# The first attention of a fused four-layer network: front work of a group of images moved beside the units of the group before

## The reference, cut to what matters

```python
q = grouped_proj(query, Wq).reshape(b, s, N_HEAD, D_HEAD) * SCALE
k = grouped_proj(query, Wk, bk).reshape(b, s, N_HEAD, D_HEAD)
v = grouped_proj(query, Wv, bv).reshape(b, s, N_HEAD, D_MODEL // N_HEAD)
content_score = jnp.einsum('bind,bjnd->bnij', q + r_w_bias * SCALE, k)
r_head = jnp.einsum('td,dnh->tnh', position_embeds, r_kernel)
pos_score = jnp.einsum('bind,tnd->bnit', q + r_r_bias * SCALE, r_head)
pos_score = rel_shift_gather(pos_score, s, shift=1)
attn_prob = jax.nn.softmax(content_score + pos_score, axis=-1)
attn_vec = jnp.einsum('bnij,bjnd->bind', attn_prob, v).reshape(b, s, D_MODEL)
h = query + (attn_vec @ Wo + bo)
mu = jnp.mean(h, axis=-1, keepdims=True)
var = jnp.mean(jnp.square(h - mu), axis=-1, keepdims=True)
return (h - mu) * jax.lax.rsqrt(var + EPS) * gamma + beta
```

## Time and profile before

| what | value |
|---|---|
| median of 3 runs | 1729.89 us (1724.44 to 1731.71) |
| the profiled execution, its own time | 1731.45 us |
| its span | 1729.6 us |
| TensorE busy with matmuls | 1444.7 us (84% of the span) |
| VectorE, ScalarE, GpSimd busy | 683.8, 669.8, 379.3 us |
| mean granted TensorE clock | 0.895 of full speed |

### The profile page before, as it was taken

How to read it: one execution, slowest core, us unless ns; L and a number is a source line. 1 busy time by engine, 2 the same in 40 slices (tenths; PEclk the granted TensorE clock), 3 DMA queues, 4 the chain that set the end, 5 groups by cost and what they waited for, 6 DMA issues and landing times.

```text
span 1729.6 us, 31842 instructions
## 1 busy us (share of the span) xinstructions
PE 1444.7 (84%) x10300; PEld 1045.9 (60%) x10300; DVE 683.8 (40%) x2107; ACT 669.8 (39%) x2209; POOL 379.3 (22%) x456
## 2 busy tenths in 40 slices
PE   6888788467687768788899899789999999889994
PEld 4555555343222335566667889656666777689994
DVE  5545655631101156544442722244442423461113
ACT  2666766120000033577753112145555542213331
POOL 5212212100000022322210156411211200024441
PEclk9898998568767868899999989989999999989997
DMA  8522523619999530000000566400000020026553
GB/s 216 142 70 69 138 60 79 223 42 345 319 305 287 166 103 1 1 0 0 0 0 0 137 194 197 142 6 1 0 0 0 5 123 0 19 75 205 184 174 101
DMA packets 94432, 178.64 MB, mean 103 GB/s; under 512 B 35578, under 2 KB 54168, under 8 KB 92704
## 3 DMA queue, kind: packets, MB, share of 16 engines
q1 hardware_dynamic: 80144, 130.65, 26.1%
q10 hardware_dynamic: 7056, 30.67, 5.5%
q0 software_dynamic: 7136, 16.10, 2.9%
HBM read 150.39 MB, written 26.99 MB: 103 GB/s over the span
## 4 chain that ended last, share of the span: by engine, by line
PE 55%; issue 14%; DMA 12%; DVE 10%; ACT 5%; SPq 2%; POOL 1%; DVEq 0%; ACTq 0%; POOLq 0%
PE bank L1762 14%; DMA WM<-in_fc 8%; PE bank L2231 6%; PE bank L2217 4%; PE bank L1852 4%; PE bank L1864 4%; PE bank L1881 3%; PE bank L1891 3%; PE bank L2221 3%; PE bank L1941 2%; PE bank L1828 2%; ACT ON L1573 1%; PE bank L2148 1%; DMA pos_scratch<-AREA 1%; ACT PB L1573 1%
## 5 line engine op out<-in xcount | busy, mean ns | idle before, releaser
L1762 PE MATMUL bank<-XT,AREA 96*128 96x408 f32 (+1 forms) x640 | 238.3, 530 | 33.4 <-ACT XT L1527 16.1
L1762 PEld LDWEIGHTS bank<-XT,AREA 96*128 96x128 f32 (+1 forms) x640 | 121.4, 196 | 139.3 <-issue 99.6
L1852 PE MATMUL bank<-KZ,QT 128*102 128x102 f32 x1152 | 145.8, 268 | 16.3 <-ACT PB L1573 6.3
L645 POOL TENSOR_TENSOR RS<-VE,expo 102x4 f32<-102x4 f32 (+1 forms) x53 | 53.0, 1000 | 433.7 <-DVE VE L855 325.6
L1852 PEld LDWEIGHTS bank<-KZ,QT 128*102 128x102 f32 x1152 | 126.5, 180 | 31.7 <-issue 13.6
L661 POOL TENSOR_TENSOR PB<-PB,RCU 102x306 f32<-102x306 f32 x96 | 66.8, 696 | 288.0 <-DVE RCU L916 287.7
L2231 PE MATMUL bank<-WM,KZ 128*128 x660 | 118.2, 327 | 0.0
L2231 PEld LDWEIGHTS bank<-WM,KZ 128*128 128x128 f32 x660 | 105.7, 190 | 0.4
L1554 ACT ACTIVATE KZ<-bank,AREA 128x128 f32<-128x128 f32 x198 | 54.6, 374 | 121.8 <-PE bank L2221 121.8
L1864 PE MATMUL bank<-AREA,OT 128*102 128x192 f32 x384 | 88.4, 343 | 15.4 <-DVE SLOTS L1133 5.4
L1881 PE MATMUL bank<-PT,V 102*32 102x102 f32 (+1 forms) x1152 | 86.0, 270 | 16.2 <-DVE OT L926 13.3
(11 more groups left out here) (312 smaller groups left out, 2769.7 us busy)
## 6 DMA issues: line engine op xcount, KB each, us to landing
AREA<-in_fc SPq DMA_DIRECT2D x10, 1536.0 KB, 20.2
SLOTS<-in_m3w SPq DMA_DIRECT2D x33, 384.0 KB
WM<-in_fc ACTq DMA_DIRECT2D x5, 2304.0 KB, 19.6
WM<-in_fc SPq DMA_DIRECT2D x6, 1536.0 KB, 19.5
AREA<-in_fc ACTq DMA_DIRECT2D x4, 2304.0 KB, 20.5
SLOTS<-in_m1w SPq DMA_DIRECT2D x33, 256.0 KB
AREA<-pos_scratch SPq DMA_DIRECT2D x16, 459.0 KB
pos_scratch<-AREA SPq DMA_DIRECT2D x8, 913.5 KB
```

Source lines behind the costliest of these rows:

```text
L1762: last = pe.matmul(dst, lhsT, rhs, start=n == 0, stop=n == len(pieces) - 1)
L1852: last = pe.matmul(psum[k][0:T, cols(j)], QT[:, tile, cols(bb)], KALL[:, unit % per_tile * (HEADS // per_tile) + tile, cols(bb)], start=Tr ...
```

## The change

Rows, queries and the position products of the first two images of the next group are made beside the units of this group, and its keys in the steps after the last unit's scores:

- step 6: the transposes of XN, and XT; steps 7, 8 and 9: two query tiles each; steps 10 to 15: two pairs of position products each (images 0 and 1 of the next group); steps 16, 17 and 18: two key tiles each. All of it goes through the two banks `XBANKS`.
- Only QR is made out of the bank. QT can't be overwritten while scores are still to be made, so VectorE makes it in steps 16 to 18 from QR, by adding a column of differences (`DQ`, the scaled r_w less r_r). `queries_ready` tells TensorE.
- TensorE waits for `scores_taken` (VectorE's add has read the bank) where it waited for `exp_ready`.
- `begin_a0`, `turn_a0` and `keep_a0` stand at steps 2, 4 and 6. GpSimd takes the power of the layer norm ahead of unit 2's probabilities, not unit 4's.
- `finish_0(g-1)` comes behind the move of V and ahead of the units.
- Each load of position scores waits for `pos_used`, now signalled by a marker instruction behind the add.
- The first group's front is written out ahead of the loop; the last group has nothing beside its units but its own images 2 and 3. What is left between two groups is `front()`: the values, and the waits for the keys' banks and for `queries_ready`.

The core of the diff:

```diff
+TURN_AHEAD, QUERIES_AHEAD, POS_AHEAD, KEYS_AHEAD = 6, (7, 8, 9), (10, 11, 12, 13, 14, 15), (16, 17, 18)
...
@@ SyncE
-                    if bb < 2:
-                        sp.wait_ge(sem["pos_used"], at.now("pos_used"))
-                    else:
-                        sp.wait_ge(sem["pos_used"], at.take("pos_used"))
+                    sp.wait_ge(sem["pos_used"], at.take("pos_used"))
...
@@ GpSimd
-                probabilities((4,))
+                probabilities((2,))
...
@@ VectorE, minima
+                    give(ins, "scores_taken")
+                    dve.wait_ge(sem["scores_taken"], at.now("scores_taken"))
                     if unit == UPB - 1:
-                        give(ins, "pos_used")
-                        dve.wait_ge(sem["pos_used"], at.now("pos_used"))
-                    else:
-                        step(ins)
+                        mark("pos_used")
...
@@ VectorE, between
+                        if s == 2:
+                            begin_a0(g + 1)
                         if s == 4:
-                            begin_a0(g + 1)
+                            turn_a0(g + 1)
                         if s == 6:
-                            turn_a0(g + 1)
-                        if s == 8:
                             keep_a0(g + 1)
...
+                        if s in QUERIES_AHEAD:
+                            queries_ahead(2 * QUERIES_AHEAD.index(s))
...
+                        if s in KEYS_AHEAD:
+                            keys_ahead(2 * KEYS_AHEAD.index(s))
...
+            def keys_ahead(first):
+
+                for p in (first, first + 1):
+                    last = ts(QT[:, p, :], QR[:, p, :], DQ[:, p:p + 1], None, ALU.add)
+                if first == 4:
+                    give(last, "queries_ready")
+                for p in (first, first + 1):
+                    keys(p)
...
             for g in range(NG):
                 at.first_banks()
...
+                values(V, 16, bv0)
                 if g:
                     finish_0(g - 1)
-                for p in range(6):
-                    keys(p)
-                values(V, 16, bv0)
                 attention(16, True, lambda bb, o, k: free(tt(a_of(g)(bb), o, a_of(g)(bb), ALU.add), k),
                           between_groups(g))
...
@@ ScalarE
+            def beside_ahead(s):
+
+                beside(s)
+                if s == TURN_AHEAD:
+                    turned(XT)
+                if s in QUERIES_AHEAD:
+                    for p in range(2 * QUERIES_AHEAD.index(s), 2 * QUERIES_AHEAD.index(s) + 2):
+                        queries(p)
+                if s in POS_AHEAD:
+                    pos_rows(POS_AHEAD.index(s) // 3, 2 * (POS_AHEAD.index(s) % 3), 2)
+                if s in KEYS_AHEAD:
+                    for p in range(2 * KEYS_AHEAD.index(s), 2 * KEYS_AHEAD.index(s) + 2):
+                        keys(p)
...
+            with at.loop(act, NG - 1):
+                attention(beside_ahead)
+            attention(beside)
...
@@ TensorE
-                            pe.wait_ge(sem["exp_ready"], at.take("exp_ready"))
+                            pe.wait_ge(sem[scores_read], at.take(scores_read))
...
+                    if s == TURN_AHEAD:
+                        pe.wait_ge(sem["xn_ready"], at.take("xn_ready"))
+                        turned.extend(turn_group(XN, halves))
+                        fresh.append(True)
+                    if s in QUERIES_AHEAD:
+                        n = 2 * QUERIES_AHEAD.index(s)
+                        if n == 0:
+                            moved(*turned)
+                        q.extend(project(wq0, p6) for p6 in (n, n + 1))
+                    if s in POS_AHEAD:
+                        n = POS_AHEAD.index(s)
+                        if n == 0:
+                            moved(*q[2:4])
+                        if n == 2:
+                            moved(*q[4:6])
+                        pos(n // 3, 2 * (n % 3), 2)
+                    if s in KEYS_AHEAD:
+                        n = 2 * KEYS_AHEAD.index(s)
+                        for p6 in (n, n + 1):
+                            project(wk0, p6)
...
+            def front():
...
+                for k in XBANKS:
+                    pe.wait_ge(sem[f"bank_free{k}"], at.now(f"bank_full{k}") + 1)
+                pe.wait_ge(sem["queries_ready"], at.take("queries_ready"))
+                return v_moved
...
+            with at.loop(pe, NG - 1):
+                v_moved = front()
+                attention(2, 16, wo0, v_moved, beside_ahead())
+            v_moved = front()
+            attention(2, 16, wo0, v_moved, beside)
```

189 lines of the change are left out of this document (97 added, 92 removed).

## The result

The changed kernel takes 1740.24 us (median of 20 runs, 1732.51 to 1745.85) against 1729.79 us (20 runs, 1720.76 to 1739.88) of the kernel before: a ratio of 1.005, 95% interval 1.0034 to 1.0065. It is slower by 10.5 us; the prediction said faster by 8.7.

The account below looks back on a forecast made before the run. Bound taken: a store-and-load chain of position scores, about 10.5 us, ending the wait at each group's start. Three periods gave -8.2 us, with -1.0 and +0.5 -8.7: 1721.2 us from a median of 1729.89; range 1707 to 1736.

Parts of the forecast that it names:

- A: Last output projection's start to the next group's second position-product batch: +12.3 in place of +24.9 us, -12.6.
- B: Second batch of position products to the scores of unit 6: +0.5 us on 12.4.
- C: Scores of unit 6 to unit 10, with transposes and query products added: 11.6 us against 9.9, +1.7.
- D: Unit 10 to unit 15, with position pairs added: 2.6 us a step, 13.0 against 10.0, +3.0.
- E: Drain, unit 15's scores to the last output projection: 14.1 us against 8.2, +5.9; bounds +2.3 and +7.5.
- the forecast case: Whole kernel: change of -2 to -15 us, time 1715 to 1728 us; chance 0.50.
- R2: Slow TensorE clock enters steps 6 to 10 or 16 to 18: +19.5 us, 1741 us; chance 0.20.
- The first front: First group's front, two banks and no overlap of queries with products: +0.5 us, between 0 and +2.
- The wait for scores: TensorE may write scores once VectorE has read the bank: -1.0 us in the last group, bounds 0 and -3.
- QT: VectorE's six SBUF passes a group making QT: 0.6 us each, bounds 0.37 and 0.64.

Follow-up runs that it names:

- e_finish: Changed kernel with the second layer norm spread over steps 11, 13 and 14 of the next group: 1732.65 us, 1.0019 of the kernel before.
- e_warm: Changed kernel with eight unread filler products on TensorE in step 17, VectorE's order unchanged: 1731.98 us, 0.9987 of the kernel before.
- e_drain: Changed kernel with VectorE's copy of OT first in the drain, keys ahead of QT, both a step later: 1727.0 us, 0.9989 of the kernel before.
- e_all2: Changed kernel with old first front, copy of OT first, second layer norm spread over steps 11, 12 and 13: 1716.41 us, 0.9916 of the kernel before.
- e_bank4: Changed kernel with its new first front through four banks in place of two: 1744.32 us in a single execution.
- e_exp: Changed kernel with the old wait for exp_ready in place of scores_taken in the first attention: 1744.26 us in a single execution.
- e_front_drain: Changed kernel with the old first front and VectorE's copy of OT first in the drain: 1724.14 us, 0.9937 of the kernel before.
- e_front: Changed kernel with the first group's front as before the change (four banks, QT from the bank): 1738.65 us, 1.0051 of the kernel before.

## Why the prediction was wrong

**A held.** Forecast 12.3 us with `finish_0` ending the wait; measured 13.29, 14.20 and 12.12, with the forecast's rows in the forecast's order. The position load is no longer in the way (e_finish: with the layer norm gone from there, 6.1). The excess over 12.1 is the slow clock behind a drain: projection 2.25 and values 2.73 us at the second boundary, against 1.22 and 1.59 of the earlier trace rows. At the first boundary the drain itself was at 1.00, and the clock fell behind t0.

**B, C and D held.** B 11.5, 13.2 and 12.8 (forecast 12.9), C 11.36 (11.6), D 12.71 (13.0). Over three groups they are 2.8 us better than forecast. D's 2.54 a step is TensorE's own sum: it is busy for 12.70 of 12.70 us in each of the three, at a clock of 1.00.

**E failed, in two parts.** Forecast 14.1 (bounds 10.5 and 15.7), measured 15.33, 18.00 and 16.61: 7.6 us too much over three drains, and two of the three above the bound. The first part is the chain's size. The step "and only then the copy of OT, at +6.2; values of unit 12 wait for it, and key product 2 behind them ends at +7.7" had the mechanism right: the copy starts at +6.66, the values at +7.2. But product 2 was counted alone, where it is issued as a pair with 3, and the moves behind it follow later than counted: 15.33 at a clock of 1.00, +1.2 a group. The second part is the clock, which the forecast case left at 1.00: 2.7 and 1.3 us in the drains, and 3.2 in the three A segments behind them, some 7 us in all. The 4.0 in the drains come from the idle time of 1.90 us (e_warm, e_drain); the 3.2 in A only in part, since 1.6 of them stay in e_drain and 2.5 in e_warm, which have no such idle time. In the drains that is rival R2's mechanism in the second place that R2 named, "product 2 of the keys"; with A it comes to a third of R2's price. The place in step 7 never showed it, and the packed steps 10 to 15 stayed at 1.00, so R2 as it was priced was not what happened: that its 1741 lies next to the result is luck. The Trainium skill, "TensorE: Matmul & The Clock Gate", "A second HAM failure mode: psum-queue depth-cycling", tells of brief idles between groups of matmuls that make the clock swing; here the clock fell behind single idles of 1.90 us in some of the drains, and of 1.74 us in e_all2, which agrees. The prediction had set it against rows which showed the low level only behind stalls of 3.3 us, and concluded too much from their silence.

**The first front failed.** +0.5, with bounds 0 ("it ends under the same load of position scores") and +2; measured +8.4, of which 0.7 is a later start. The bound left out what two banks do to twelve pairs of position products (a product waits for its bank's move every time, 1.53 us in place of 0.92 a batch) and that this is TensorE's path, not covered by a load that lands at 57. The prediction did name it as what would lie outside its terms, and e_bank4 shows the banks to be 6.7 us of the front. The same two banks cost nothing in steps 10 to 15, since there other products fill the wait.

**The wait for scores: right size, wrong cause.** The last group is 1.0 shorter, as forecast, but e_exp shows that the new signal has no part in it. What else made it is not known; a layer norm that no longer ends inside the front and a different start of the group are candidates, and neither was tried. Part of it may be spread: over six profiles whose last group differs in nothing but e_exp's wait, and whose last E is 8.36 (the changed kernel, its repetition, e_drain, e_warm, e_front_drain, e_exp), it takes from 41.6 to 42.3 us.

**Left out: what a shift does to the clock behind the stage.** The +3.0 between the last t0 and the reload is in no term. The distance from the last t0 to the reload is 85.2 us or more in nine of the twelve profiles of the changed and edited kernels, and within 1 us of before's 82.3 in e_warm, e_bank4 and e_all2. What decides when the clock comes back is open: no run set the moment on purpose.

**QT.** The forecast took 0.6 us a pass. The line of the changed kernel (count, ns min/median/max, first and last start, forms):

```profile
L1112 DVE TENSOR_SCALAR QT<-AREA,DQ x24: 419/427/968, 52.3 to 245.0; 128x408 f32<-128x408 f32 x24
```

0.43, two thirds of the 642 ns of the earlier trace rows. The rule that the prediction cites from the Trainium skill ("VectorE: DVE Perf Modes", "Mode 2×_2P"), twice the rate, agrees with the 427 ns in kind: the pass is shorter, if not by half. My slope from a pass with 192 elements was wrong. It changed little: 0.2 us a pass is 0.4 in each E chain, 1.2 over three groups, and the chain in E was long for another reason.

By account: predicted -8.7 at the reload, measured +9.5, a difference of 18.2. The first front has 7.9 of it, the periods 7.3 (E +7.6, A +2.7, B to D -2.8; the rest is rounding), the clock behind the stage 3.0.

## What to carry to other kernels

In a drain, where units no longer hide each other, order each engine's instructions by who waits for them: a copy that frees TensorE comes ahead of long passes which are only needed later, and one such order was worth 12 us here. When work is moved to a place with fewer banks, count the bank's round (product, hand-off, move, hand-off) for the copy of that code that has nothing beside it, such as the first group's. And judge a repair with the others in place: while short idles are left that drop TensorE's clock, a gain of 8 us elsewhere can measure as 1, as it did here.

## What the runs showed of the hardware that was not expected

- Which drains lose the clock comes out alike in kernels with the same start, and differently with another start. The same instructions behind the same idle time of 1.9 us took 15.3, 18.0 and 16.6 us in the changed kernel, 15.3, 18.1 and 16.7 in its repetition and 15.3, 17.9 and 16.6 in e_exp; where unit 0's scores start 8 to 9 us earlier, 17.8, 16.6 and 19.4 (e_front) and 18.0, 16.6 and 19.4 (e_bank4). Without the idle time (e_drain, e_warm) all three are alike. Whether the moment at which a drain begins decides this, or what ran ahead of it, is not shown.
- Shorter idles can do it too. In the six kernels without the idle time of 1.9 us in the drains, the clock fell behind t0 at eight of eighteen boundaries, at a cost of 1.1 to 1.6 us each; in e_drain nothing longer than 0.61 and 0.98 us of idle time stood ahead of it.
- In the experts' first products the clock came back 3.4 us after the start of their first row in the kernel before, and 15.7 us after it in the changed kernel, in the same code.
- Two QT passes took 1.31 us where they ran beside a multiplication on GpSimd (the first of them 968 ns, the second 422), and 0.78 without it (e_drain). All three drains of the changed kernel, of its repetition and of e_warm show this, at 967 to 970 ns. GpSimd's timeline of the changed kernel at the same moment:

```profile
170.79 0.70 POOL L657 TENSOR_TENSOR ON<-ON,RCU 102x306 f32<-102x306 f32 x1 [0.60 <-DVE RCU L911]
```

  The multiplication itself takes 0.70, as always. The Trainium skill, "SBUF — State Buffer", "SBUF: two separate sides", says that a VectorE pass in the two-port mode named above and a GpSimd instruction take a shared pair of ports by turns, each for a whole instruction; the 0.55 us that the first pass is longer agrees with one that waits for most of GpSimd's 0.70.
